# A transformer block on one core: the attention's output products take four PSUM banks in turn instead of two

## What is computed

```python
def _layernorm(x, axis=-1, eps=1e-05): ...
def _L0_attn_ref(x, Wq, Wk, Wv, Wo):
    q = jnp.einsum('bse,ef->bsf', x, Wq)      # k, v alike
    attn_scores = jnp.einsum('bes,bfs->bef', qT, kT) / np.sqrt(HEAD_DIM)
    attn_weights = jax.nn.softmax(attn_scores, axis=-1)
    attn_output = jnp.einsum('bef,bfs->bes', attn_weights, vT)
    return jnp.einsum('bse,ef->bsf', jnp.swapaxes(attn_output, 1, 2), Wo)
def _L0_ffn_ref(hidden_states, gate_cp, up_cp, down_cp):
    ...                                        # weights are splines of control points
    inter = jax.nn.silu(gate) * up
    return jnp.einsum('bsi,hi->bsh', inter, down_w)
x = L0_attn_x
x = x + _layernorm(_L0_attn_ref(_layernorm(x), ...))
x = x + _layernorm(_L0_ffn_ref(_layernorm(x), ...))
```

## Time and profile before

| | |
|---|---|
| runs of the kernel | 815.83, 817.82, 820.35 us (median 817.82) |
| profiled execution, its time | 813.27 us |
| its span | 811.4 us (clock 0.972 on the mean) |
| PE busy | 740.7 us, 91% |
| DVE, POOL, ACT busy | 529.2, 440.0, 373.7 us (65%, 54%, 46%) |
| the 384 matmuls of the y tiles (three lines) | 51.8 + 50.0 + 49.9 us busy |

### The profile page before, as it was taken

The page is one execution under the profiler, slowest core; times in us unless marked ns, Lnnn a source line. Parts: engine busy times, 40 slices in busy tenths (PEclk is TensorE's granted clock), DMA queues, the critical chain, the costliest instruction groups (busy, mean ns, idle before and its releaser), DMA issues. The chain is left out here.

```text
span 811.4 us, 19045 instructions
## 1 busy us (share of the span) xinstructions
PE 740.7 (91%) x7152; PEld 507.3 (63%) x7152; DVE 529.2 (65%) x1025; ACT 373.7 (46%) x635; POOL 440.0 (54%) x615
## 2 busy tenths in 40 slices
PE   6987999999999999799767899999989999999996
PEld 3665767787787768587533366565656556565565
DVE  7674763686458744565656668778767787865453
ACT  3531332343233333132446666666656666666541
POOL 5289749185854669311335446555545455455542
PEclk9897899999999999899989999999999999999999
DMA  6725447144732456502871515455353544536313
GB/s 239 267 81 174 155 165 239 55 149 133 231 126 77 142 194 235 111 2 88 271 249 57 192 59 169 140 163 178 124 178 93 180 160 131 171 105 192 109 53 105
DMA packets 64314, 120.55 MB, mean 149 GB/s; under 512 B 12144, under 2 KB 28656, under 8 KB 62192
## 3 DMA queue, kind: packets, MB, share of 16 engines
q1 hardware_dynamic: 64240, 119.53, 45.2%
HBM read 82.94 MB, written 36.57 MB: 147 GB/s over the span
## 5 line engine op out<-in xcount | busy, mean ns | idle before, releaser
L1260 POOL TENSOR_TENSOR act<-inter,act 128x512 f16<-128x512 f32 x128 | 158.5, 1249 | 127.2 <-ACT act L1301 127.2
L1374 DVE SCALAR_TENSOR_TENSOR inter<-ubank,c_up,gated 128x512 f32<-128x512 f32 x128 | 95.9, 749 | 74.9 <-ACT gated L1305 74.2
L1514 PE MATMUL ybank<-down,act 128*128 128x160 f16 x512 | 110.4, 235 | 0.0
L1515 PE MATMUL ybank<-down,act 128*128 128x160 f16 x512 | 109.5, 233 | 0.0
L1516 PE MATMUL ybank<-down,act 128*128 128x160 f16 x512 | 109.5, 233 | 0.0
L1305 ACT ACTIVATE gated<-gbank,c_gate 128x512 f32<-128x512 f32 x128 | 87.8, 686 | 45.3 <-PE gbank L1473 45.3
L1301 ACT CAST act<-inter 128x512 f16<-128x512 f32 x128 | 78.9, 617 | 48.8 <-DVE inter L1374 48.8
L1514 PEld LDWEIGHTS ybank<-down,act 128*128 128x128 f16 x512 | 50.1, 98 | 39.2 <-issue 35.5
L1473 PE MATMUL gbank<-z,s_twice 128*32 128x512 f16 x512 | 51.8, 395 | 9.5 <-PEq L84 4.3
L748 PE MATMUL ybank<-ga_hi,xT_hi 128*128 128x512 f32 x128 | 51.8, 404 | 6.1 <-ACT shared L539 4.4
L539 ACT ACTIVATE shared<-ybank,yr 128x512 f32<-128x512 f32 x32 | 22.0, 688 | 72.0 <-POOL yr L363 72.0
(11 more groups left out here) (192 smaller groups left out, 2076.2 us busy)
## 6 DMA issues: line engine op xcount, KB each, us to landing
x_ln<-x SPq DMA_DIRECT2D x64, 256.0 KB, 3.5
z<-token_features SPq DMA_DIRECT2D x16, 1024.0 KB, 5.4
job<-job_in SPq DMA_DIRECT2D x24, 640.0 KB, 4.1
shared<-x SPq DMA_DIRECT2D x32, 256.0 KB, 2.8
x<-shared SPq DMA_DIRECT2D x32, 256.0 KB, 2.0
token_features<-z_hi SPq DMA_DIRECT2D x64, 128.0 KB
token_features<-z_lo SPq DMA_DIRECT2D x64, 128.0 KB
x_res<-x SPq DMA_DIRECT2D x32, 256.0 KB, 2.8
```

The source lines that it names most:

```text
L1260: pool.tensor_tensor(hidden[par][:, i, TOK:2 * TOK], inter[:, i % INTERS, :], hidden[par][:, i, 0:TOK], ALU.subtract).then_inc(inter_ready, 1)
L1374: dve.scalar_tensor_tensor(out=inter[:, i % INTERS, :], in0=ubank[:], scalar=c_up[:], in1=gated[:, i % 2, :], op0=ALU.mult, op1=ALU.mult). ...
L1514: pe.matmul(out, hidden[par][:, r, high], box[:, 0], start=False, stop=False)
L1515: pe.matmul(out, hidden[par][:, r, high], box[:, 1], start=False, stop=False)
```

## The change

The y tiles take four banks in turn, the two of `ybank` and then the two of `tbank`. ACT and DVE read them there. Tile 2, the first in `tbank`, waits until the transpositions of this batch have been copied out; tiles 4 to 7 wait for the tile four before. `mirror(b, 0)` of every batch but the first waits for all eight normalisations of the batch before, because it writes `tbank` again. All else stands as it was.

```diff
+        y_banks = [ybank[:, 0, :], ybank[:, 1, :], tbank[:, 0, :], tbank[:, 1, :]]
...
-                    act.activation(y_n[:, t % 2, :], ybank[:, t % 2, :], ACT.Copy,
+                    act.activation(y_n[:, t % 2, :], y_banks[t % 4], ACT.Copy,
...
-                        dve.bn_stats(ystats[:, t % 2, :], ybank[:, t % 2, :]).then_inc(y_bn, 1)
+                        dve.bn_stats(ystats[:, t % 2, :], y_banks[t % 4]).then_inc(y_bn, 1)
...
                 pe.wait_ge(lo_done, b * EVACS + m + 1)
+                if m == 0 and not (isinstance(b, int) and b == 0):
+                    pe.wait_ge(y_normed, b * NT)
...
                 for t in range(NT):
-                    if t >= 2:
-                        pe.wait_ge(y_normed, b * NT + t - 1)
+                    if t == 2:
+                        pe.wait_ge(tb_hi, (b + 1) * TB)
+                        pe.wait_ge(tb_lo, (b + 1) * TB)
+                    if t >= 4:
+                        pe.wait_ge(y_normed, b * NT + t - 3)
...
-                        mm = product(ybank[:, t % 2, :], xT_hi[:, k, c], xT_lo[:, k, c], m_hi[:, k, :],
+                        mm = product(y_banks[t % 4], xT_hi[:, k, c], xT_lo[:, k, c], m_hi[:, k, :],
                                      m_lo[:, k, :], k == 0, k == K - 1)
```

## The result

The changed kernel takes 809.74 us (median of 13 runs, 805.0 to 812.99) against 817.82 us before (13 runs, 811.13 to 821.07). The ratio is 0.9903, with a 95% interval of 0.9876 to 0.993, so it is faster by 0.7 to 1.2%. The forecast was 810.0 us. The profiled execution of the change has a span of 805.4 us, 6.0 us less than the profiled one of before.

What follows compares the result with a forecast made beforehand. The prediction took the kernel's y-tile stages to be bound by a ring with too few banks, PE and DVE waiting in turn; 7.39 us from three batches plus 0.4 from the last gave 810.0 us, range 806.5 to 814.5.

Steps and rivals of the forecast that it cites:

- The ring of two banks: y tiles, batches 0 to 2: with four banks PE runs through, stages last 21.76 us, 7.39 us gained in all.
- The rival that the chain's rate limits: y tiles: PE still waits at tiles 4 to 7 despite four banks; 815.0 us, chance 0.05.
- Reaching the next batch: Stage end into the next batch: POOL and the others move with PE, so the whole saving is kept.
- The mirror's wait: Mirror 0, behind two Gram blocks: 5.7 us of cover hides the wait for the last normalisation; cost 0.
- the prediction's rival: Mirror 0: last normalisation comes after the second Gram block, PE stands three times; 822 us or more, slower chance 0.03.
- The last batch: Last batch to block end: tile 4's statistics 0.9 us earlier; gain 0 to 0.9, taken as 0.4, DMA queues being full.
- The clock: y-tile stages: granted clock already 1.00 despite the stalls, so removing them gives no clock back.
- the prediction's rival, a longer stand at the barrier that costs clock: Before transposition and barrier: PE's longer stand lowers the clock, costing 4.8 us again; 814.8 us, chance 0.07.
- The sum: Whole kernel: 7.39 + 0.4 = 7.8 us gained, median 817.82 to 810.0 us.

Runs made afterwards that it cites:

- the second profiles: The kernel before, profiled again (span 810.7 us), and the unaltered change profiled once more in its repeat measurement (810.22 us, ratio 0.9923).
- the second comparison: The unaltered change measured once more against the kernel before, beside two variants on one chip: 810.22 us, ratio 0.9923 (0.9894 to 0.9951).
- the first comparison: The change against the kernel before, 13 runs each: 809.74 against 817.82 us, ratio 0.9903 (0.9876 to 0.993).

## Why the prediction was right, and where a term was off

**The ring of two banks.** Right to the hundredth: 21.76 us in all three batches, no wait for ACT, 2.72 us between statistics. Three banks do it as well, as the 3.2 us of holding against 2 x 2.72 us say. The rival that the chain's rate limits has fallen with this.

**Reaching the next batch.** Right. The first y matmuls of batches 1, 2 and 3 came 2.05, 4.57 and 8.39 us earlier. From the first Gram matmul of batch 1 to its y tiles it takes 63.97 us against 64.04 before, so nothing is given back. The 1.19 us of the last batch's third square are not the change's either: the kernels of this document that run the same program up to there have it last 18.2 to 19.6 us, at a mean granted clock of 0.84 to 0.85 where it is short (up to 18.4 us) and 0.82 to 0.83 where it is long (19.4 and more). POOL moved along as argued: PE's wait for the softmax in front of that square, which POOL sets (DVE stands 7.2 us for POOL's `hr` before it starts on the softmax, at 325.90 us), was 3.74 us before and 3.65 with the change.

**The mirror's wait.** Right, 0: no wait for ACT shows anywhere among PE's waits. Its price without cover was too low in the prediction's rival: 3.35 us of standing and 1.4 to 2.9 us of a lower clock behind it for each, where the prediction counted the standing alone. The cover of two Gram blocks is what makes this change pay. The same change with the wait two Gram blocks earlier ends 0.3% slower than the kernel before.

**The last batch.** This is the term that was mis-sized: 0.4 us gained, between 0 and 0.9. The reasoning up to the transposition held: DVE's statistics of tile 4 at 379.80 are 13.93 us behind the first y matmul where they were 389.13 - 374.26 = 14.87 us behind it, 0.94 us earlier against the forecast 0.9, and the last store was issued 0.9 us earlier. First the issue of the 1024 KB load before, then, with the change, the statistics of tile 4, the load and the last store (403.54 in the earlier trace rows):

```profile
398.33 0.37 SPq L1082 DMA_DIRECT2D z<-token_features  x1
```

```profile
379.80 0.70 DVE L673 BATCH_NORM_STATS2 ystats<-ybank 128x6 f32<-128x512 f32 x1
...
389.60 0.37 SPq L1088 DMA_DIRECT2D z<-token_features  x1
...
394.24 0.33 SPq L289 DMA_DIRECT2D x<-shared  x1
```

What the prediction had wrong is what follows the store's issue. Its lower bound of 0 took it that transfers issued at the same time or earlier can't end later. They did. From issue to landing, the load took 5.8 us before and 6.4 with the change, the last store 3.8 us before and 4.9 with the change:

```profile
z<-token_features SPq DMA_DIRECT2D x1, 1024.0 KB, 5.8
```

```profile
z<-token_features SPq DMA_DIRECT2D x1, 1024.0 KB, 6.4
```

```profile
x<-shared SPq DMA_DIRECT2D x1, 256.0 KB, 3.8
```

```profile
x<-shared SPq DMA_DIRECT2D x1, 256.0 KB, 4.9
```

In the second profiles it was 5.9 us for the load before and 8.2 with the change. The landings also show how the load holds the end. In all nine profiles with the load at its old place, the stores issued behind it land behind it, in the order of their issue; the last of them lands 3.1 to 3.2 us behind the load, and the feed-forward block's first matmul comes 0.8 us behind that, although the last store was issued anywhere from 27.1 to 29.3 us behind the first y matmul. So an earlier last store gains nothing there. In the four profiles with the load one step earlier the last store lands 2.3 us behind its own issue, and then compute and the residuals set the end.

How large the term is, is less sure. The three profiles with two banks in the last batch have end stretches of 33.80, 32.99 and 32.99 us, the two of the change 34.03 and 35.18, and the four others with three or four banks and the load at its old place 34.13 to 35.94. By the first five the term is a loss of about 1.4 us (0.2 to 2.2), outside its bounds. The whole time doesn't resolve it: the kernel with two banks in the last batch has the ratio 0.9904, the change 0.9903 and 0.9923. That the load and the stores around it are the limit is shown by moving the load both ways. Why the load lands later with more banks is not shown; no run took the transfers apart.

**The clock.** Right for the stages: the granted clock is 1.00 in all three, with the stalls and without them. The Trainium skill's rule on cycling through banks ("TensorE: Matmul & The Clock Gate", section "A second HAM failure mode: psum-queue depth-cycling"), that brief idles between groups make the clock swing, is not borne out by the stalls of this kernel, and nothing extra came. Outside the stages the prediction's rival, a longer stand at the barrier that costs clock, is not excluded: in the second comparison the mean granted clock was 0.967 with the change and 0.970 before. The difference is within the scatter of single runs (0.962 to 0.973 and 0.964 to 0.979), and is worth 2.3 us at most, as an estimate (0.0028 of 810 us). The profiles don't settle it: around the barrier the granted clock was 0.83 in both of the change, and 0.91 and 0.83 in the two of before.

**The sum.** 7.39 us minus about 1.4 is 6.0, the forecast 7.8; measured were 7.9 us by the ratio of the first comparison (5.7 to 10.1) and 6.3 us by that of the second (4.0 to 8.6). Both values lie in both intervals, so the time can't tell the sum with the loss from the sum without it. That the forecast of 810.0 came within 0.3 us of 809.74 is luck: the last term was off by some 2 us, and the runs of one kernel lie 8 to 10 us apart.

## What to carry to other kernels

A ring of buffers is sized by comparing how long a buffer is held behind its producer's turn (here 3.2 us, read off two rows) with (banks - 1) times the producer's period (2.72 us): here two banks were too few (3.2 against 2.72), three enough (against 5.44), and a fourth was spare. Banks may be borrowed from a neighbouring stage if the wait that gives them back has work in front of it; look at what is queued there first, because here an uncovered stand cost itself and then the clock behind it. At the end of a block with a barrier, ask whether the last stores stand behind a large load; here they landed only behind it, and compute that came earlier was worth nothing. Try moving the load, and watch what comes to stand behind it.

## What was not expected of the hardware

After a stand of PE of 3.2 us the granted clock fell to the lower level (1.2 GHz) three times out of three, and so it did at the stand of 3.65 us in front of the last batch's third square in the change (0.50 from 330.0 to 336.7 us). Behind the first of them matmuls of 128x512 fp16 lasted 0.60 us instead of 0.38, at a granted clock of 0.57 in the 4 us around them; after stalls of 0.4 to 0.8 us in the kernel before the clock stayed at 1.00. A 256 KB store issued at the block's end kept SP waiting 1.3 us when no large load was under way, 1.9 to 2.0 us with a 1024 KB load issued 8 us or more ahead of it, and 2.6 to 6.1 us behind one issued 3.6 to 6.2 us ahead of it.
